# Summing four heads with two additions instead of one strided reduction

## The reference

```
xt    = (x @ weight).reshape(-1, 4, 64)
alpha = softmax(leaky_relu(alpha_l + alpha_r, 0.01), axis=1)     # four numbers per edge
tmp   = einsum('nh,nhd->nd', alpha[:n], xt[col[:n]])             # sum over the four heads
x     = layernorm(x + tmp repeated for the four heads)
```

## Time and profile before

| | |
|---|---|
| median of three runs | 2377.72 us |
| profiled execution | 2377.29 us |
| its span | 2375.5 us |
| TensorE busy, over the span | 2208.2 us (93%) |
| VectorE busy | 2132.9 us (90%) |
| ScalarE busy | 1927.9 us (81%) |
| GpSimd busy | 1641.4 us (69%) |

### The profile page before, as it was taken

How to read it: one execution, slowest core, us unless ns; L and a number is a source line. 1 busy time by engine, 2 the same in 40 slices (tenths; PEclk the granted TensorE clock), 3 DMA queues, 4 the chain that set the end, 5 groups by cost and what they waited for, 6 DMA issues and landing times. The chain is left out here.

```text
span 2375.5 us, 50565 instructions
## 1 busy us (share of the span) xinstructions
PE 2208.2 (93%) x12061; PEld 1809.9 (76%) x12061; DVE 2132.9 (90%) x6133; ACT 1927.9 (81%) x4051; POOL 1641.4 (69%) x1693
## 2 busy tenths in 40 slices
PE   7499799999999999999999999999999999999988
PEld 6255588887888888887888888878888888878867
DVE  6587699999999999999999999999999999999967
ACT  3477588888888888888888888888888888888857
POOL 1671477777777777777777777777777777777730
PEclk9699899999999999999999999999999999999999
DMA  7698799999999999999999999999999999999964
GB/s 281 164 242 284 244 283 282 279 282 272 281 280 280 284 281 285 279 280 274 282 282 281 284 281 280 282 273 284 278 280 283 283 280 282 278 279 279 282 203 146
DMA packets 300661, 642.52 MB, mean 270 GB/s; under 512 B 63260, under 2 KB 120976, under 8 KB 300632
## 3 DMA queue, kind: packets, MB, share of 16 engines
q0 software_dynamic: 129840, 418.70, 60.0%
q1 hardware_dynamic: 168888, 217.10, 30.5%
q10 hardware_dynamic: 1904, 6.40, 0.7%
HBM read 583.36 MB, written 58.64 MB: 270 GB/s over the span
## 5 line engine op out<-in xcount | busy, mean ns | idle before, releaser
L954 POOL DMA_INDIRECT e_kv<-kv_tab,e_idx x1568 | 1532.5, 977 | 489.7 <-issue 442.1
L1083 ACT ACTIVATE e_gate_ps<-e_gate_ps 128x1024 f32<-128x1024 f32 x786 | 765.6, 1002 | 247.7 <-PE e_gate_ps L1015 247.6
L1155 DVE TENSOR_TENSOR e_gated<-e_kv,e_gate_ps 128x1024 f32<-128x1024 f32 x788 | 932.0, 1210 | 26.7 <-issue 19.5
L1002 PE MATMUL e_sum_ps<-e_gated,weighed_hot 128*128 128x256 f32 x3168 | 749.1, 379 | 2.1 <-ACT weighed_hot L1099 2.1
L1014 PE MATMUL e_gate_ps<-wd_hi_lo,high 128*128 128x512 f32 x1572 | 639.3, 407 | 92.7 <-DVE e_gated L1155 92.1
L1002 PEld LDWEIGHTS e_sum_ps<-e_gated,weighed_hot 128*128 128x128 f32 x3168 | 600.1, 190 | 98.5 <-ACT weighed_hot L1099 2.7
L1015 PE MATMUL e_gate_ps<-wd_bias,low 128*128 128x512 f32 x1572 | 620.2, 395 | 0.0
L1164 DVE CUSTOM_DVE_ANT_0 e_gated<-e_gated,e_q_ps 128x256 f32<-128x256 f32 x1576 | 571.4, 409 | 1.0 <-PE e_q_ps L1034 1.0
L1099 ACT ACTIVATE weighed_hot<-hot,e_attn 128x128 f32<-128x128 bf16 x1580 | 520.1, 401 | 41.1 <-DVE e_attn L1174 32.9
L1014 PEld LDWEIGHTS e_gate_ps<-wd_hi_lo,high 128*128 128x128 f32 x1572 | 296.2, 188 | 224.0 <-issue 90.4
L1033 PE MATMUL e_q_ps<-q_win,hot_t 128*128 128x256 f32 x1572 | 424.0, 303 | 0.6 <-DVE e_dot L1164 0.6
(11 more groups left out here) (159 smaller groups left out, 1332.6 us busy)
## 6 DMA issues: line engine op xcount, KB each, us to landing
e_attr<-attr_groups_dram SPq DMA_DIRECT2D x784, 128.0 KB
e_q_next<-q_tab SPq DMA_DIRECT2D x98, 256.0 KB
e_kv<-kv_tab,e_idx POOLq DMA_INDIRECT x1568
sum_tab<-e_sums SPq DMA_DIRECT2D x100, 128.0 KB
e_prior<-sum_tab SPq DMA_DIRECT2D x99, 128.0 KB
kv_tab<-l_kv_out SPq DMA_DIRECT2D x49, 256.0 KB, 4.8
q_tab<-l_q_out SPq DMA_DIRECT2D x49, 256.0 KB, 3.7
sum_tab<-zeros SPq DMA_DIRECT2D x25, 256.0 KB, 2.8
```

Of the source, the lines that this page charges most:

```text
L954: pool.indirect_dma_start(kv[:, k, :], None, kv_tab, bass.IndirectOffsetOnAxis(ap=idx[:, at:at + 1], axis=0)).then_inc(kv_landed[k // G][k ...
L1002: last = nc.tensor.matmul(sum_ps[:, 0:H], weighed_hot[:, c % 2, k, :], gated[:, c * G + k, H:2 * H], start=(c == 0 and k == 0), stop=(c == ...
L1083: nc.scalar.activation(gate_ps[:, 2 * p:2 * p + 2, :], gate_ps[:, 2 * p:2 * p + 2, :], ACT.Silu).then_inc(silu_ready[s][p], 1)
L1155: nc.vector.tensor_tensor(gated[:, pair(s, p), :], kv[:, pair(s, p), :], gate_ps[:, 2 * p:2 * p + 2, :], ALU.mult).then_inc(gated_ready[s] ...
```

## The change

The reduction over the heads, one instruction that reads 256 columns with a stride and writes 64, is replaced by an addition of the halves (columns 0 to 127 and 128 to 255) into a new tile `halved`, and an addition of the halves of that into `mixed`. The two stand in neighbouring steps of the pipeline, so the pipeline of `mix` is one step longer, later operations of a tile stand one step later, and the second `low_q` inside `mix` goes from step 5 to step 6. `scores` and `centre` of the next chunk keep their step.

```diff
@@ -450,6 +450,7 @@
         inverted_total = sb("inverted_total", [P, 2, C], F32)
         alpha = sb("alpha", [P, 2, C, HEADS], F32)
         weighed = sb("weighed", [P, 3, H], F32)
+        halved = sb("halved", [P, 3, 2 * DH], F32)
         mixed = sb("mixed", [P, 3, DH], F32)
         stats = sb("stats", [P, RING, 6], F32)
         mean_var = sb("mean_var", [P, CHUNKS, C, 2], F32)
@@ -473,8 +474,8 @@
         src_landed, dst_landed = sems("src_landed", CHUNKS), sems("dst_landed", CHUNKS)
         scored, leaked, topped, centred, exped, totalled, inverted, alpha_ready = (
             sem(n) for n in ("scored", "leaked", "topped", "centred", "exped", "totalled", "inverted", "alpha_ready"))
-        weighed_ready, mixed_ready, sum_ready, normed_ready = (
-            sem(n) for n in ("weighed", "mixed", "sum", "normed_ready"))
+        weighed_ready, halved_ready, mixed_ready, sum_ready, normed_ready = (
+            sem(n) for n in ("weighed", "halved", "mixed", "sum", "normed_ready"))
         stat_ready, var_ready, padded, first_inverse, unit_ready, unit_padded, unit_inverted, inverse_ready, rstd_ready, shift_ready = (
             sem(n) for n in ("stat", "var_ready", "padded", "first_inverse", "unit_ready", "unit_padded", "unit_inverted", "inverse_ready",
                              "rstd_ready", "shift_ready"))
@@ -682,7 +683,7 @@
 
                 def mix(g, meanwhile):
                     n = SIZES[g]
-                    for i in range(n + 4):
+                    for i in range(n + 5):
                         if i < n:
                             t = STARTS[g] + i
                             if i == 0:
@@ -693,24 +694,28 @@
                         if 0 <= i - 1 < n:
                             t = STARTS[g] + i - 1
                             dve.wait_ge(weighed_ready, t + 1)
-                            nc.vector.tensor_reduce(mixed[:, t % 3, :], weighed[:, t % 3, :].rearrange("p (h d) -> p d h", h=HEADS), AX.X, ALU.add).then_inc(mixed_ready, 1)
+                            nc.vector.tensor_tensor(halved[:, t % 3, :], weighed[:, t % 3, 0:2 * DH], weighed[:, t % 3, 2 * DH:], ALU.add).then_inc(halved_ready, 1)
                         if 0 <= i - 2 < n:
                             t = STARTS[g] + i - 2
+                            dve.wait_ge(halved_ready, t + 1)
+                            nc.vector.tensor_tensor(mixed[:, t % 3, :], halved[:, t % 3, 0:DH], halved[:, t % 3, DH:], ALU.add).then_inc(mixed_ready, 1)
+                        if 0 <= i - 3 < n:
+                            t = STARTS[g] + i - 3
                             dve.wait_ge(mixed_ready, t + 1)
                             if t % 5 == 0:
                                 dve.wait_ge(x_landed[t // 5], 16 * x_loads(t // 5))
                             nc.vector.tensor_tensor(x_sb[:, t, :].rearrange("p (h d) -> p h d", h=HEADS),
                                                     x_sb[:, t, :].rearrange("p (h d) -> p h d", h=HEADS),
                                                     mixed[:, t % 3, :].unsqueeze(1).broadcast_to([P, HEADS, DH]), ALU.add).then_inc(sum_ready, 1)
-                        if 0 <= i - 3 < n:
-                            t = STARTS[g] + i - 3
+                        if 0 <= i - 4 < n:
+                            t = STARTS[g] + i - 4
                             dve.wait_ge(sum_ready, t + 1)
                             nc.vector.bn_stats(stats[:, t % RING, :], x_sb[:, t, :]).then_inc(stat_ready, 1)
-                        if 0 <= i - 4 < n:
-                            t = STARTS[g] + i - 4
+                        if 0 <= i - 5 < n:
+                            t = STARTS[g] + i - 5
                             dve.wait_ge(stat_ready, t + 1)
-                            last = nc.vector.bn_aggr(mean_var[:, g, i - 4, :], stats[:, t % RING, :])
-                        if i in (2, 5):
+                            last = nc.vector.bn_aggr(mean_var[:, g, i - 5, :], stats[:, t % RING, :])
+                        if i in (2, 6):
                             queries(meanwhile[i // 4:i // 4 + 1])
                         if i == min(4, n) and EARLY <= g and g + 1 < CHUNKS:
                             scores(g + 1)
```

## The result

| | before | after |
|---|---|---|
| median | 2377.72 us (9 runs, 2375.37 to 2380.58) | 2370.73 us (9 runs, 2365.63 to 2376.17) |
| profiled execution | 2377.29 us | 2365.63 us |
| its span | 2375.5 us | 2363.8 us |

The ratio is 0.9972, with the interval 0.9963 to 0.9981. The kernel became 7.0 us faster, 0.3%, where 3.3 us were forecast; the range ended at 2371.2.

A forecast was written before the change was run, and what follows sets the result against it. The second stage was taken as bound by a 15.40 us VectorE-ScalarE loop per chunk, guarded by gathers. Gains of 3.88 us, 3.3 after lengthened gathers, gave 2374.0 for the profiled execution and 2374.4 for the median; range 2371.2 to 2377.6.

The forecast's parts named there:

- `layer0` as a sum: Second stage: 0.68 us up to chunk 6 plus 3.20 from chunks 7 to 10, 3.88, about 3.3 after lengthened gathers.
- the part ahead of chunk 7: Second stage: gather landings cancel savings of chunks 0 to 4; chunk 5's shift comes 0.34 us earlier, chunk 6's 0.68.
- slowed gathers: GpSimd in the second stage: the new two-input additions lengthen gathers, 0.6 us by chunk 7's landing, bounds zero and twice that.
- The pitch: VectorE in `mix`: starts 0.21 and 0.14 us behind the two additions against 0.51, saving 0.16 per tile, 0.80 per chunk.
- rival 2: VectorE in `mix`: each short addition holds the engine its whole duration, 0.51 us together, nothing saved, 2377.7 us; chance 0.12.
- Where the gathers hold: Second stage: VectorE asks 1.53 us earlier, beyond margins of 1.1 and 1.4, so scores of chunks 6 and 7 wait.
- their own obstacles don't matter: Chunks 0 to 4: whatever they save is lost at chunk 5's wait for gathers landing at 142.0, so their hindrances count nothing.
- Rival 1: Second stage: gathers don't hold; chunks 4 to 10 give 5.6 us, about 6.2 with the first chunks, 2371.5 us; chance 0.14.
- TensorE's waits: Second stage: once-per-chunk stops for a ScalarE copy, 1.06 to 1.20 us, shrink by 0.80 to 0.3 to 0.4, chunks 7 to 10.
- hits in proportion, half the hold each: GpSimd: 13 lengthened gathers scaled by the new additions' hold over 0.66 us, each costing half the hold, 0.6 us in all.
- rival 3: GpSimd: additions systematically catch gather starts; 0.15 us on each of 64 makes it 5.7 slower, 2383.4 us; chance 0.04.

The follow-up runs named there:

- +128: 128 instructions more ahead of the edge loop: before with 128 memsets 2381.87 us (ratio 1.0011), after with 79 more memsets 2378.54 us (1.0001).
- +49: 49 instructions more ahead of the edge loop: before with 49 memsets, 2373.61 us (ratio 0.9988), repeated at 2373.14 us (0.9985); also the place of after.
- +64: After with 15 memsets more, the edge loop 64 instructions further than in before: 2369.12 us, ratio 0.9967.
- +0: The kernel before, no instructions added ahead of the edge loop: 2377.72 us.
- +1: Before with one memset more ahead of the edge loop: 2378.32 us, ratio 0.9998.
- +24: Before with 24 memsets ahead of the edge loop: 2379.57 us, a single execution.
- +96: Before with 96 memsets ahead of the edge loop: 2378.75 us, a single execution.

## Why the prediction came out as it did

**The failed step** is "The edge stage and the last one keep their instructions, so the question is by how much `layer0` ends earlier; I carry that over to the end one to one". The instructions were kept, their place in VectorE's list was not, and at 98 back edges VectorE idled 0.19 to 0.20 us each before and 0.08 us after. That is a second gain beside that of `layer0`, and the forecast had put it at nothing. Padding alone brings it, padding behind the loop doesn't, and at +128 it is gone. In eleven profiled executions with the short rhythm the 99 `e_sums` span 2004.4 to 2008.5 us, in seven with the long one 2011.7 to 2015.0, 6.5 us apart in the mean. The timed medians give the place 3.2 and 4.4 us. Both are less than 98 times 0.11, or 10.8 us. Part of it goes back into waits of `e_gated` for gathers, 7.4 to 10.8 us in the eleven (mean 9.0) and 3.5 to 7.3 in the seven (mean 5.2). From 300 to 2250 us of after TensorE is busy for 97%, VectorE and the DMA engines for 95%, so none of them has much to give.

**`layer0` as a sum.** 3.3 us were forecast. The medians at equal places differ by 2.8 and 3.3; each ratio is uncertain by some 2 us either way, so each difference by about 3. The profiles give less: the last matmul ends 1.4 us earlier on average (251.64 in eight with the list of before, 250.24 in seven with that of after, two of which are the runs with later scores and with nine buffers; without these two it is 250.21). The first profile, with 3.47, is the best of the seven, so nothing finer than "1.4 to 3.3" is shown, and that the sum was right is not. What it had wrong is the part ahead of chunk 7. The shift of chunk 6 was to come 0.68 us earlier, or 0.1 after the slowed gathers; over the same profiles it comes 2.0 us later (165.6 against 163.5; only in the first profile it was level). The four chunks behind it give 3.4, for 3.20.

**The pitch.** Forecast 0.21 and 0.14 us, measured 0.20 and 0.14 (once 0.17); durations 0.29 and 0.22 forecast, 283 and 215 ns measured. A full chunk gained 0.86 us, by the distance of the shifts, for 0.80. The next start comes 0.08 us ahead of the end, also for these narrow additions, so rival 2 is out. The Trainium skill, VectorE: DVE Perf Modes, section "The DRAIN you can't avoid", says that the next operation waits until the pipe is empty, and adds that one which is not held starts earlier. The prediction named the first half alone; the rows show no such wait.

**Where the gathers hold** was one chunk off. I had the scores of chunks 6 and 7 waiting, by 0.5 to 2.5 us. It was those of 5 and 6, by 2.19 and 0.52 in the first profile and by 2.77 and 1.71 in the third. In all seven profiles the scores of chunk 5 waited, for 2.2 to 3.9 us, and in four of them those of chunk 6. My argument that "their own obstacles don't matter" for the chunks ahead looked at the wait in chunk 5 alone. For chunk 7 I expected 156.54 and a landing at 157.0; the last gather landed at 148.3 + 8.4 = 156.7, and VectorE, held up before, came at 157.68 and didn't wait. So in the first profile the gain up to chunk 6 was 0.04 rather than 0.68, and the four chunks behind it gave 3.43 where I had 3.20. Rival 1 is wrong as well. No run shows its 6.2 us: without the source gathers, at the same place, the two `layer0` differ by 3.0 us in the medians (2372.58 and 2369.62) and by 3.45 in the profiles, and the nine buffers were not tried with the old `layer0`.

**TensorE's waits** fell to 0.23 to 0.34 in chunks 8 to 10, for 0.3 to 0.4 forecast, and to none in chunks 6 and 7, since it had a backlog from the 4.29 us that it stood still in chunk 5.

**Slowed gathers** was the term too small. The time by which the first 64 of GpSimd's issues exceed the usual 0.945 us sums to 1.9 to 2.8 us in eight executions with the list of before (mean 2.2) and to 2.4 to 5.0 in seven with that of after (mean 3.9): 1.6 us more, not 0.6. Issues of over 1.0 us are no more in number (9 to 14 in both). The difference is one to three single issues: none with the old list took over 1.21 us, while with the new one an issue near 90 us took 1.71 in all seven, one near 111 us 2.04 in five, and one near 126 us 2.00 in two. The issue near 90 us before and after, and that near 126 us in the third profile of after:

```profile
89.59 0.94 POOL L503 DMA_INDIRECT l_by_src<-xt_tab,score_idx  x1 [0.30 <-issue]
```

```profile
89.64 1.71 POOL L504 DMA_INDIRECT l_by_src<-xt_tab,score_idx  x1 [0.30 <-issue]
```

```profile
126.17 2.00 POOL L504 DMA_INDIRECT l_by_src<-xt_tab,score_idx  x1 [0.30 <-issue]
```

So "hits in proportion, half the hold each" was wrong in kind. The long issue of after falls on a stretch in which VectorE runs eight instructions with two inputs one behind the other (88.64 to 90.46), where before a reduction with one input starts at 89.55 and another at 90.39. That would be the mechanism of rival 3, at single places instead of everywhere; no run tests it apart. The slowed issues are a part of what the scores of chunk 5 wait for: the last gather for chunk 5 was issued at 122.46 instead of 121.55. At 1.6 us for 64 gathers their cost stays below the 3.9 from which rival 3 would decide. The stores land later too. The page of after lists for `kv_tab` and `q_tab` 6.4 and 5.5 us, that of before 4.8 and 3.7:

```profile
kv_tab<-l_kv_out SPq DMA_DIRECT2D x49, 256.0 KB, 6.4
q_tab<-l_q_out SPq DMA_DIRECT2D x49, 256.0 KB, 5.5
```

## What to carry to other kernels

A change in one stage can move another stage through the length of an engine's instruction list; before a difference of 0.2% in a kernel with a loop is put down to an edit, pad the list of before by as many instructions, or compare a visit of the loop in both traces. For a multi-input sum, count distances between starts, not durations: two halving additions of 128 and 64 columns held VectorE 0.34 us, the strided reduction 0.51. And behind a guard stands the next: with gathers taken away, the stage waited for stores.

## What the runs showed of the hardware

The cost of VectorE's back edge depends on where the loop lies. At +49 and +64 it idled about 0.08 us per visit, at +0, +1, +24, +96 and +128 0.19 to 0.23. The step that changes is the one from the taken branch to the next recorded instruction: 0.19 us at +49 and +64, 0.30 at +0, +1 and +24, 0.32 at +96 and +128. Which property of the place decides is open.

The Trainium skill, Runtime: NRT & Kernel Launch, section "Instruction fetch mechanics", says that instructions are fetched in order in blocks of 256, and that a taken branch whose target lies outside the two blocks at hand stalls until the target's block has been fetched by DMA. The rows don't fit a fetch per visit. The instruction queues move 10 and 19 packets in the whole execution, before as after, against 98 back edges:

```profile
q8 instruction: 10, 0.16, 0.0%
q14 instruction: 19, 0.16, 0.0%
```

and a loop of some 90 instructions (the trace records 88 per visit, control instructions counted) that is slow when it crosses a block's end would have one stretch of slow places, at most some 90 wide, in 256; the slow places found lie on both sides of a fast stretch and span 128. I varied only the place, so a fetch from inside the engine, or an alignment of another kind, is neither shown nor excluded.
